# Attention scores: three PSUM banks for the scores by token and two for the scores by set, in the middle of the stream

## The reference, cut to what matters

```
K, V   = sums of k, v over sets of 4, 8, 16, ... tokens   # 512 slots stand for the sets
logits = q . K * scale, masked to sets that ended at or before the token
tail   = q . (sum of k over the token's own unfinished set of 4) * scale
att    = softmax(logits, tail)          # 16 heads of 16 channels
out    = att @ V + att_tail * V_tail;   x = x + out @ W_proj.T
```

## Time and profile before

| | us |
|---|---|
| median of 3 runs | 1905.24 (1900.28 to 1913.64) |
| the profiled execution | 1906.12 |
| its span, first to last instruction | 1904.4 |
| mean granted TensorE clock | 0.899 |
| TensorE busy | 1528.0 (80%) |
| VectorE, ScalarE busy | 958.7, 711.6 |

### The profile page before, as it was taken

One profiled execution on the slowest core, in us unless ns is written; L12 is line 12 of the kernel. 1 busy time (PEld: TensorE's weight loads), 2 busy tenths in 40 slices (PEclk: granted clock), 3 DMA queues, 4 the chain that ended last, 5 costly groups with the idle time before them and its releaser, 6 DMA issues. The chain is left out here.

```text
span 1904.4 us, 26989 instructions
## 1 busy us (share of the span) xinstructions
PE 1528.0 (80%) x9510; PEld 1142.5 (60%) x9510; DVE 958.7 (50%) x2602; ACT 711.6 (37%) x1741; POOL 571.0 (30%) x463
## 2 busy tenths in 40 slices
PE   1789979999999578349999997389993559998993
PEld 1656634454544454238888987255552549888893
DVE  5676477777774395764431111256555744421110
ACT  0122226656566376325423222013333425322321
POOL 2443030000000342202446464322101231545436
PEclk9889989999999898558999999699995569999997
DMA  3014372414210022304768784510114016788765
GB/s 97 17 72 119 119 136 56 92 36 86 37 45 2 1 100 78 149 13 136 238 186 243 215 240 97 134 34 23 45 56 168 9 45 197 224 228 226 230 180 55
DMA packets 114066, 212.60 MB, mean 112 GB/s; under 512 B 20149, under 2 KB 79962, under 8 KB 104730
## 3 DMA queue, kind: packets, MB, share of 16 engines
q1 hardware_dynamic: 87066, 178.93, 29.4%
q0 software_dynamic: 26880, 32.13, 11.3%
HBM read 158.71 MB, written 51.90 MB: 111 GB/s over the span
## 5 line engine op out<-in xcount | busy, mean ns | idle before, releaser
L908 DVE TENSOR_REDUCE attnm_top<-psum 128x1 f32<-128x384 f32 (+3 forms) x384 | 216.0, 598 | 67.7 <-PE psum L997 62.7
L1132 ACT ACTIVATE attnm_prob<-psum 128x512 f32<-128x512 f32 (+1 forms) x384 | 192.4, 530 | 130.0 <-PE psum L1007 124.8
L2186 POOL DMA_INDIRECT out<-moe2e_y,moe_scatter_i x80 | 125.5, 1568 | 164.3 <-ACT moe2e_y L2323 97.4
L2186 POOL DMA_INDIRECT x_sum<-moe1e_y,moe_scatter_i x80 | 126.3, 1579 | 156.2 <-ACT moe1e_y L2323 85.6
L2243 PE MATMUL psum<-moe2e_xgT,moe_w_up 128*128 128x160 f32 x1024 | 155.0, 311 | 10.8 <-issue 8.4
L2369 DVE SCALAR_TENSOR_TENSOR moe2e_h<-moe2e_gate,psum 128x160 f32<-128x160 f32 x160 | 50.6, 321 | 220.7 <-ACT moe2e_gate L2296 220.5
L2369 DVE SCALAR_TENSOR_TENSOR moe1e_h<-moe1e_gate,psum 128x160 f32<-128x160 f32 x160 | 50.6, 321 | 214.3 <-ACT moe1e_gate L2296 214.1
L2243 PE MATMUL psum<-moe1e_xgT,moe_w_up 128*128 128x160 f32 x1024 | 152.2, 307 | 7.2 <-issue 4.8
L2243 PEld LDWEIGHTS psum<-moe2e_xgT,moe_w_up 128*128 128x128 f32 x1024 | 148.0, 198 | 13.8 <-issue 13.8
L2243 PEld LDWEIGHTS psum<-moe1e_xgT,moe_w_up 128*128 128x128 f32 x1024 | 145.2, 195 | 10.3 <-issue 10.3
L1301 POOL DMA_INDIRECT moe_xg<-xn_rows,moe_gather_i x80 | 83.6, 1045 | 152.5 <-issue 73.0
(11 more groups left out here) (414 smaller groups left out, 3193.3 us busy)
## 6 DMA issues: line engine op xcount, KB each, us to landing
moe_w_up<-in_expert_up SPq DMA_DIRECT2D x64, 1024.0 KB, 5.7
moe_w_down<-in_expert_down SPq DMA_DIRECT2D x64, 512.0 KB, 6.9
attnm_q_hat<-q_parts SPq DMA_DIRECT2D x72, 128.0 KB, 4.7
moe_a_up<-in_adapter_up SPq DMA_DIRECT2D x32, 256.0 KB, 6.9
q_parts<-attnf_q_part SPq DMA_DIRECT2D x12, 512.0 KB, 2.8
attnm_k_hat<-k_parts SPq DMA_DIRECT2D x72, 64.0 KB, 2.3
x_res<-in_x SPq DMA_DIRECT2D x8, 512.0 KB, 8.5
v_tails<-attnf_v_tail SPq DMA_DIRECT2D x4, 1024.0 KB, 3.9
```

Source lines behind the costliest of these rows:

```text
L908: nc.vector.tensor_reduce(top[:, n // QUADS % 2, tiles[0]:tiles[-1] + 1, hh:hh + 1], s.ps[:, u.bank, 0:len(tiles) * width].rearrange("p (t ...
L1132: nc.scalar.activation(prob[:, i % NPROB, at:GROUP], s.ps[:, u.bank, at:GROUP], ACT.Exp).then_inc(taken[u.bank], 1)
L2186: nc.gpsimd.indirect_dma_start(total, bass.IndirectOffsetOnAxis(ap=scatter_i[:, at:at + 1], axis=0), y[:, q, k, :], None, bounds_check=TOK ...
```

## The change

It changes which bank a score group of the middle stream uses, nothing else: A groups from step 2 on go round banks 0, 1 and 2, and B groups up to quad 13 alternate between banks 3 and 4. No instruction is added, removed or moved in any engine's order; the numbers of the semaphores and the counts waited for follow from the banks.

```
         if kind == "A":
-            u_a[q, h, t] = banks.use(na % (5 if q < 2 else 2))
+            u_a[q, h, t] = banks.use(na % (5 if q < 2 else 3))
             na += 1
         elif kind == "B":
 
-            u_b[q, h, t] = banks.use(2 + nb % 3 if q < NQ - 2 else nb % 5)
+            u_b[q, h, t] = banks.use(3 + nb % 2 if q < NQ - 2 else nb % 5)
             nb += 1
```

## The result

The changed kernel takes **1894.28 us** (median of 9 runs, 1883.27 to 1898.13) against 1905.24, a ratio of 0.9929 with a 95% interval of 0.9911 to 0.9948: 11 us less. Forecast were 1895.8 us in a range of 1887 to 1906, so the forecast held.

What follows compares the result with a forecast made beforehand. TensorE was taken as the bound, its A groups waiting for VectorE's maxima with two banks. Four plain steps at 0.34 and ten at 0.9 give 10.4 us, less 1: 1905.24 - 9.4 = 1895.8 us, range 1887 to 1906.

Steps and rivals of the forecast that it cites:

- What bounds the stream: Middle stream, 290 to 592 us: TensorE's A groups wait for VectorE's maxima, 15 to 17 us in all.
- The plain step: Stream step without output work: 0.82 us of old waits, 0.48 us of new ones, gain 0.34 us; four such steps.
- The output steps: Ten stream steps where VectorE also does normalisation and update: gain 0.6 to 1.2 us each, 0.9 in the middle.
- Step 8: Stream step with output work: its time was to fall from 26.39 to about 25.2 us.
- the new wait does not appear: Steps with output work: no new wait of B groups for ScalarE's exponential where that work parts two B groups.
- the worst place: VectorE's backlog in step 8: of an A group's 1.06 us wait, 0.57 gained, 0.49 moved to the next group.
- ScalarE's other copies: B groups queued behind ScalarE's copies at L1098: 1 us taken off the summed gain, not gone through.
- ScalarE is never late: B groups in the stream always find a free bank, so the kernel takes 1889 us; chance 0.14.
- two banks bind the B groups: Third B group of blocks with 512-wide exponentials: new waits exceed those removed, 3 us slower, 1908 us; chance 0.10.
- the waits are not for the bank: A groups wait for something that moves along, such as the mask and its weight load: 1905 us; chance 0.06.
- the fourth rival: New small pauses bring the 1.2 GHz clock for one stream step, about 18 us more, 1914 us; chance 0.02.

## Why the prediction was right

**What bounds the stream** held. In steps 3 to 15, taking each A group's start against the shortest distance that the same pair of groups shows anywhere in the stream, the A groups had waited 18.1 us; "15 to 17" was a little low. They wait 2.8 us now, all but 0.2 of it in steps 7, 8, 11, 12 and 15, where the wait for VectorE moved on by one group.

**The plain step** held term by term: gain 0.34 forecast, 0.33 measured in steps 3 and 5 and 0.46 in step 4, whose A groups had waited 0.14 us more. Against the kernel with a third bank for both, the gain is made of 0.89 removed and 0.56 added, where 0.82 and 0.48 were forecast. The waits of over 0.02 us in a plain step, counted by starts, come to 0.82 and 0.49, the forecast's own figures; the other 0.07 us, in both terms, are spread over distances that are each longer by less than 0.02 us, and fall out of the difference.

**The output steps** were mis-sized: 0.9 us each in the middle, and 1.10 measured (12.2 less three plain steps is 11.0, over ten): 0.82 in steps 6, 10 and 14, 1.37 to 1.39 in the five heaviest, 1.04 in 9 and 0.64 in 13. Step 8 was to fall to about 25.2 and fell to 25.01. The step that was off in size is this estimate, which was never added up from blocks. Measured as above, the A groups of these ten steps had waited 1.5 us each, 0.3 us of that moved on, and new waits of B groups take 0.2. The forecast had remarked that the new wait does not appear where output work stands between two B groups, and had not counted it: B groups wait 0.02 us in steps 7, 8, 11, 12 and 15, 0.4 in 6, 10 and 14, and 0.5 in all others. At the worst place it was too high instead (0.57 us, where 0.33 were gained), and the smaller waits, which go entirely, outweigh that: in step 8 they are 1.0 us. The 1 us taken off for ScalarE's other copies was not called for either; no step shows it. Together these terms make 9.0 us for steps 3 to 15 by the forecast (three plain at 0.34, ten at 0.9, less 1) against 12.2. The median moved by 11.0, since the part ahead of step 3 and the scatter of executions weigh as much as that difference. So the 9.4 us forecast for the whole came near the 11.0 by luck in part: the steps gave 3 us more than their sum, and 1.0 us of it was lost again ahead of them.

**The rivals.** That ScalarE is never late is refuted by the 0.56 us above. That two banks bind the B groups is refuted as a net loss (1.0002 with A's gain left out) but is near: with one bank the same waits cost 28.56 - 18.85 = 9.7 us in a plain step, seventeen times the 0.56. That the waits are not for the bank is refuted by the block rows. The clock stayed granted in full (1.00) over steps 3 to 15 with the change, with the new pauses in them, so the fourth rival did not come true; but it was no idle fear. With one bank for the B groups the pauses, 0.2 to 0.5 us ahead of most B groups, did come with the lower level in the middle of the stream, at 3.6 us in step 4. The change's new pauses are of at most 0.19 us. By "Perfetto Trace Analysis" of the Trainium skill (section Matmuls) independent groups should rotate through banks; the trace agrees for the A groups, and the experiment with one round of five shows that whom a bank comes from counts as much as how many there are: 18.93 against 19.41 us with the same five.

## What to carry to other kernels

Of two consumers that share a pool of banks, give the spare bank to the one for which the producer waits, and before that work out one block by starts, releases and the consumer's duration: here that arithmetic was right to 0.02 us in each block of a plain step. A wait removed in front of a late engine moves on to the next group, so only the part up to that group's own earliest start is gained, and less where the producer has gained time already on the way there (0.33 us instead of 0.57 here). A common round over both kinds of group can be better than a split where both consumers keep up (18.93 against 19.41 us in a plain step); where one falls behind, the split keeps the other going (25.01 against 25.40 in step 8). And a bank too few can cost more than its waits: with one bank for the B groups the clock fell too.

## What had not been expected of the hardware

How long step 2 takes differs between executions by up to half of what the change gives, for two reasons, and neither is a wait for a bank. Its first B group needs the maxima of quad 0 in `attn_q_first`, which a transfer brings (L862), and TensorE stands idle until it lands. Before, after, and in the repeat of the change:

```profile
271.28 0.40 PE L1005 MATMUL psum<-attn_mask_st,ident_bf 128*128 128x256 bf16 x1 [4.06 <-DMA attn_q_first<-attnm_mT]
...
271.29 0.40 PE L1005 MATMUL psum<-attn_mask_st,ident_bf 128*128 128x256 bf16 x1 [4.82 <-DMA attn_q_first<-attnm_mT]
...
275.39 0.39 PE L1005 MATMUL psum<-attn_mask_st,ident_bf 128*128 128x256 bf16 x1 [8.02 <-DMA attn_q_first<-attnm_mT]
```

SyncE had issued that transfer by 263.9 us before and by 263.8 in the repeat, so the same 8 KB parts landed 4 us later there. During the idle time the granted clock falls to its lower level, and it is still there when TensorE starts again. The stretch at the lower level, before and after:

```profile
268.20:275.03 6.83, 3.75 (x16) 2.21 (x17) 2.54 (x9) 1.74 (x3) 0.00 (x0) 0.50 1.13 181
...
267.43:277.67 10.24, 6.38 (x28) 3.50 (x29) 4.31 (x11) 2.96 (x6) 0.00 (x0) 0.50 0.94 152
```

From the first B group to the rise TensorE works 3.8 us at 1.2 GHz before the change (271.28 to 275.03), 6.4 after it, and 5.6 in the repeat. So of the 1.8 us that step 2 is longer after the change, 0.8 are a longer wait for the transfer and 1.0 the rest of the step, with the later rise in it; of the 4.6 us in the repeat (29.5 against 24.9), 4.0 are the transfer.

Over all kernels with two or more banks for each kind of group, step 2 took 23.8 to 29.5 us, and the wait for the transfer in it 3.4 to 8.1 us. It does not go with the dealing of banks: the kernel in which only the output steps are changed deals them up to step 5 as before, and its step 2 took 27.5 us against 24.9, with 6.0 us of that wait. Every later step repeats to a few hundredths of a microsecond. Why the transfer lands late, and what sets the moment of the rise, was not tried.
